# Reordering the start of a 1-core AdaLN kernel: the first mixer group's norms, table load and modulation

## The chip, the cores and the metric

The kernel runs on one core of a Trainium2 chip. The metric is device time in microseconds (us), the median of three runs. The engines are named as in the profile: PE (TensorE matmul, PEld its weight loads), DVE (VectorE), ACT (ScalarE), POOL (GpSimd), SP (SyncE, which issues most transfers). PEclk is the granted clock of TensorE, which has two levels, 1.2 and 2.4 GHz.

## What is computed

Two AdaLN blocks over x of 2 x 1024 x 128 (float32), each "norm, modulate, mixer, gated add, norm, modulate, feed-forward, gated add". Only the first mixer's start is touched:

```python
mod = (silu(c) @ wmod).reshape(2, 6, 1, -1)          # sa, ca, ga, sb, cb, gb
h = layernorm(x) * (1 + ca) + sa
r  = sigmoid(h @ W_r.T + b_r)
ek = exp(h @ W_k.T + b_k);  v = h @ W_v.T + b_v
td, g = exp(b_td), exp(global_decay)
# scan over time
sa = ek_t*v_t + td*sa;  sb = ek_t + td*sb
wkv = (g*ek_t*v_t + sa) / (g*ek_t + sb + EPS)
# then a spiking membrane over r_t*wkv: mem, reset, spk
x = x + ga * spikes
...                                                   # local attention x2 layers, LRU, mixture of experts
```

## The kernel before, in words

The 2048 tokens lie in four groups of 512 columns (`NG = 4`, `g` from 0 to 3), channels on the 128 partitions. Each engine has its own instruction list, written out by hand in order; the only links are semaphores, so an instruction that waits holds everything behind it on its own engine.

For a mixer group g the chain of work is this:

- DVE `mixer_stats(g)`: mean and variance of four token tiles (L865, L868), then L870 and L871, which signals `ln_var`.
- POOL `ln_rstd`: reciprocal root by a power (L632, `rst`) and L633 (`nmr`), which signals `ln_rstd`.
- ACT `mixer_norm(g)` (L374, four activations into `lnx`), signals `ln_norm`.
- PE `mixer_turn(g)` turns x (L1330 on `big`) and `ln_t2` turns `lnx` (L1330 on `lnx`). ACT `mixer_x(g)` (L388) copies the first.
- ACT `mixer_out(g)` (L380) applies the modulation and writes `hsA`; for g = 0 it first waits for `mod_fin`.
- PE multiplies `hsA` by the k and v weights (L1383, L1386).
- ACT makes `ek` (L409, needs the Exp table), scales it by `sc[:,1:2]` (L412, for g = 0 waits for `sc_ready`), and makes `gek` (L414).
- DVE: L911 (`ek*v`, waits for both products and `ek_ready`), two scans (L917 for `sbb`, L919 for `sab`), L922, then the reciprocal L925. The reciprocal waits for `den_ready`, which POOL L683 signals: the sum of `gek` and `sbb`, which waits for `gek_ready` and `sb_ready` (end of L917).
- POOL after L683 of group 0: `rope_tables(0)`, four products (L642, L645), ahead of L683 of group 1.

After the four groups DVE runs the membrane passes until about 86 us; then come PE transposes, the norm and attention.

Off this chain: POOL computes the decays `sc` from `vec` with small powers (L653 to L658, which end with `sc_ready`), and L662 to L665 for the LRU. The modulation is Silu of c (ACT L365), twelve small products on PE (L1369), seven small instructions on DVE (from L887 on) that end with `mod_fin`. `warm(n)` issues n products of the identity with itself, two passes each (L1362), and their result is not used. `ident` and `vec` are the two transfers on ACT's queue (L360, L361), both counted on `ld_c`.

POOL runs the decays, then `ln_rstd` of groups 0 and 1, then L662 to L665, then `ln_rstd` of groups 2 and 3. `ln_stats` of group n waits for `ln_norm` of group n-2, since the buffers alternate.

Of the kernel before, what the change touches and what calls it, by code (L numbers as in the profile page):

```python
# [13 lines left out]
ACT = mybir.ActivationFunctionType  # L14
# [61 lines left out]
def program(nc, a, out):  # L76
    with ExitStack() as ctx:
        def sb(name, shape, dt=F32):
            return ctx.enter_context(nc.sbuf_tensor(name, shape, dt))
# [4 lines left out]
        def sem(name):  # L84
            return ctx.enter_context(nc.semaphore(name))


        ident = sb("ident", [P, P])
# [33 lines left out]
        tvec = big[:, 5, 0:T]  # L122

        ek, gek, ekv, sab, sbb, _, rsg = (big[:, i, :] for i in range(7))

        oT = big[:, 0:4, :]
# [52 lines left out]
        psT0 = ps("psT0", [P, GW])  # L179
        psT1 = ps("psT1", [P, GW])  # L180

        names = """ld_x0 ld_x1 ld_x2 ld_x3 ld_wm0 ld_wm1 ld_ew ld_c ld_wr ld_wa ld_wq ld_wl ld_lru ld_moe ld_out st_out
            init table edges mod_raw silu_c mod_mm mod_fin sc_ready
            ln_t1 ln_var ln_rstd ln_norm ln_t2 ln_out
            xT_fill xT_evac
# [9 lines left out]
        s = {n: sem(n) for n in names}  # L195
# [3 lines left out]
        def gsl(g):  # L199
            return slice(g * GW, (g + 1) * GW)  # L200

        def bof(g):
            return g // GPB
# [3 lines left out]
        def ln_no(stage, g):  # L207
            return stage * NG + g
# [22 lines left out]
        def out_bank(n):  # L231

            if n // NG == 1:
                return psO[:, 0, :]
            return psO[:, 1, :] if n >= 5 * NG and n % 2 == 0 else psT1[:, :]
# [10 lines left out]
        def out_before(n):  # L246

            return n if n < 5 * NG else n - 1
# [108 lines left out]

        @block.scalar
        def _(act):
            act.dma_start(ident[:, :], a["ident"]).then_inc(s["ld_c"], 16)  # L360
            act.dma_start(vec[:, :], a["vec"]).then_inc(s["ld_c"], 16)  # L361
            own = Steps(act, s["act_own"])

            act.wait_ge(s["ld_c"], 32)
            act.activation(silc[:, :], vec[:, V_C:V_C + 4], ACT.Silu).then_inc(s["silu_c"], 1)  # L365


            def ln_norm(n, src=None):
                act.wait_ge(s["ln_rstd"], n + 1)
                if n >= 2:  # L370
                    act.wait_ge(s["ln_t2"], n - 1)
                src = stat_bank(n) if src is None else src
                for k in range(TPG):
                    act.activation(lnx[:, n % 2, k, :], src[:, k, :], ACT.Identity, bias=nmr[:, n % 2, k:k + 1],  # L374
                                   scale=rst[:, n % 2, k:k + 1]).then_inc(s["ln_norm"], 1)


            def ln_out(n, dst, scale, bias):
                act.wait_ge(s["ln_t2"], n + 1)
                act.activation(dst, out_bank(n), ACT.Identity, bias=bias, scale=scale).then_inc(s["ln_out"], 1)  # L380


            def mixer_norm(g):
                ln_norm(ln_no(0, g), xt[:, g * TPG:(g + 1) * TPG, :])

            def mixer_x(g):
                act.wait_ge(s["xT_fill"], g + 1)
                act.activation(x_cm[:, gsl(g)], psT0[:, :], ACT.Copy).then_inc(s["xT_evac"], 1)  # L388

            def load_table(function):  # L390

                act.activation(sc[:, 9:10], half[:, 0:1], function).then_inc(s["table"], 1)

            def mixer_out(g):
                if g == 0:
                    act.wait_ge(s["mod_fin"], 1)
                b = bof(g)
                ln_out(ln_no(0, g), hsA[:, gsl(g)], mod[:, 0, CA, b:b + 1], mod[:, 0, SA, b:b + 1])

            mixer_norm(0)  # L400
            mixer_x(0)
            mixer_norm(1)
            act.wait_ge(s["init"], 2)
            load_table(ACT.Exp)
            mixer_out(0)
            for g in range(NG):

                act.wait_ge(s["kv_mm"], 2 * g + 1)
# [209 lines left out]
        def _(pool):  # L618
# [8 lines left out]
            def ln_rstd(n):  # L627

                pool.wait_ge(s["ln_var"], n + 1)
                if n >= 2:  # L630
                    pool.wait_ge(s["ln_norm"], TPG * (n - 1))
                own.one(pool.tensor_tensor(rst[:, n % 2, :], mv[:, n % 2, :, 1], half[:, 0:TPG], ALU.pow))  # L632
                pool.tensor_tensor(nmr[:, n % 2, :], nmean[:, n % 2, :], rst[:, n % 2, :], ALU.mult).then_inc(s["ln_rstd"], 1)  # L633
# [15 lines left out]

            pool.wait_ge(s["ld_c"], 32)
            own.one(pool.memset(fr[:, 0:1], float(np.e)))  # L653
            own.did(pool.tensor_tensor(sc[:, 0:1], fr[:, 0:1], vec[:, V_BTD:V_BTD + 1], ALU.pow))
            own.did(pool.tensor_tensor(sc[:, 2:3], fr[:, 0:1], vec[:, V_GD:V_GD + 1], ALU.pow))
            own.one(pool.tensor_scalar(fr[:, 1:2], vec[:, V_BTD:V_BTD + 1], 0.0, -T / 2, ALU.max, ALU.mult))
            own.one(pool.tensor_tensor(sc[:, 1:2], fr[:, 0:1], fr[:, 1:2], ALU.pow))
            pool.tensor_scalar(sc[:, 3:4], sc[:, 1:2], 1e-6, 0.0, ALU.mult, ALU.add).then_inc(s["sc_ready"], 1)  # L658
            ln_rstd(ln_no(0, 0))
            ln_rstd(ln_no(0, 1))  # L660
            for dst, src in ((4, V_NU), (5, V_TH), (6, V_GAM)):
                own.did(pool.tensor_tensor(sc[:, dst:dst + 1], fr[:, 0:1], vec[:, src:src + 1], ALU.pow))  # L662
            own.sync()
# [194 lines left out]
        def _(dve):  # L858
# [17 lines left out]
            def mixer_stats(g):  # L876

                dve.wait_ge(s[f"ld_x{g}"], 16)
                ln_stats(ln_no(0, g), xt[:, g * TPG:(g + 1) * TPG, :])

            mixer_stats(0)
            mixer_stats(1)
            dve.wait_ge(s["ld_c"], 32)
            def modulation(k, bank):

                dve.wait_ge(s[("mod_mm", "mod_raw")[k]], 1)
                own.one(dve.tensor_copy(mod[:, k, :, :], bank[:, 0:12].rearrange("p (k n) -> p k n", k=6)))  # L887
                own.did(dve.tensor_scalar(mod[:, k, CA::3, :], mod[:, k, CA::3, :], 1.0, None, ALU.add))
                gk = mod[:, k, GA::3, :]
                sgn, mag = modt[:, 0, :, :], modt[:, 1, :, :]  # L890
                own.did(dve.tensor_scalar(sgn, gk, 0.0, 2.0, ALU.is_ge, ALU.mult))
                own.one(dve.scalar_tensor_tensor(out=mag, in0=gk, scalar=-1.0, in1=gk, op0=ALU.mult, op1=ALU.max))
                own.one(dve.tensor_scalar(sgn, sgn, -1.0, None, ALU.add))
                own.one(dve.scalar_tensor_tensor(out=gk, in0=mag, scalar=0.25, in1=sgn, op0=ALU.max, op1=ALU.mult))
                dve.tensor_copy(zero[:, 0:1], mod[:, k, 0, 0:1]).then_inc(s["mod_fin"], 1)
# [430 lines left out]
        def _(pe):  # L1326
            mm = pe.matmul
            def four(dst, src):
                for k in range(TPG):
                    i = pe.transpose(dst[:, k * P:(k + 1) * P], src(k), ident[:, :])  # L1330
                return i
# [6 lines left out]
            def ln_t2(n):  # L1338
                pe.wait_ge(s["ln_norm"], TPG * (n + 1))
                if n:  # L1340
                    pe.wait_ge(s["ln_out"], out_before(n))
                four(out_bank(n), lambda k: lnx[:, n % 2, k, :]).then_inc(s["ln_t2"], 1)


            pe.wait_ge(s["ld_c"], 32)

            def mixer_turn(g):
                pe.wait_ge(s[f"ld_x{g}"], 16)
                if g:
                    pe.wait_ge(s["xT_evac"], g)  # L1350
                four(psT0, lambda k: xt[:, g * TPG + k, :]).then_inc(s["xT_fill"], 1)
# [7 lines left out]
            def warm(times):  # L1359

                for _ in range(times):
                    mm(psO[:, 0, 0:P], ident[:, :], ident[:, :], start=True, stop=True)  # L1362

            mixer_turn(0)
            pe.wait_ge(s["silu_c"], 1)
            def modulation(k, bank):
                pe.wait_ge(s[f"ld_wm{k}"], 16)
                for j in range(6):
                    i = mm(bank[:, j * 2:j * 2 + 2], wmod[:, k, j * P:(j + 1) * P],  # L1369
                           silc[:, 2 * k:2 * k + 2], start=True, stop=True)  # L1370
                i.then_inc(s["mod_mm"], 1)

            warm(6)
            modulation(0, psQK[:, 0, :])
            warm(4)

            ln_t2(ln_no(0, 0))
            pe.wait_ge(s["ld_wr"], 16)
            for g in range(NG):
                pe.wait_ge(s["ln_out"], ln_no(0, g) + 1)  # L1380
# [479 lines left out]
```

## Time and profile before

| what | us |
|---|---|
| median of 3 runs (lowest, highest) | 576.92 (576.17, 577.79) |
| the profiled execution: its own time | 577.64 |
| the profiled execution: its span | 575.7 |
| busy in the span: PE, DVE, ACT, POOL | 487.1, 445.6, 347.6, 309.3 |
| mean granted PE clock | 0.948 |

All instruction times below come from the profiled execution and count from the start of its span. A timeline row reads: start, duration, engine, line, operation, output <- inputs, count, and in brackets how long the engine was idle before it and what released it. Merged rows (x4) give the start of the first and the time to the end of the last.

### The profile page before, as it was taken

To read this page: it belongs to the slowest core of one execution; us is meant where nothing else is said; L and a number is where in the kernel's file an instruction comes from. 1 tells how busy PE (TensorE), PEld (TensorE's weight loads), DVE (VectorE), ACT (ScalarE), POOL (GpSimd) and SP (SyncE) were. 2 spreads that over 40 slices of the span, in tenths; PEclk is the share of its full clock that TensorE was granted. 3 is DMA by queue.
4 is the path that set the end of the run, shared out by engine and by line. 5 is a ranking of instruction groups with operands and counts; after the bars stand their busy time and mean duration, and the time that the engine had idled before them with its cause. 6 is when DMAs were issued, how large, how long until landed. Compare 5 with 4: busy or idle time off the path is not lost. (4 is left out here: it accounts for less than half of the span.)

```text
span 575.7 us, 11716 instructions
## 1 busy us (share of the span) xinstructions
PE 487.1 (85%) x4006; PEld 310.9 (54%) x4006; DVE 445.6 (77%) x1197; ACT 347.6 (60%) x1001; POOL 309.3 (54%) x252
## 2 busy tenths in 40 slices
PE   6541026689999999999989999999999999999995
PEld 5311013357777776543457777776544445667774
DVE  5899998998999995546799999996455687457775
ACT  4861002579999997643469999997647526533331
POOL 5651002788888888576878888885010275110000
PEclk9995558889999999999989999999999999999999
DMA  8400002011111112100021111111000000000000
GB/s 292 148 1 1 1 1 71 3 38 40 37 38 36 37 35 45 49 1 1 0 84 39 39 38 40 38 40 29 10 1 1 0 2 0 1 0 20 20 18 20
DMA packets 14194, 18.89 MB, mean 33 GB/s; under 512 B 2187, under 2 KB 8629, under 8 KB 14005
## 3 DMA queue, kind: packets, MB, share of 16 engines
q1 hardware_dynamic: 13844, 18.04, 11.7%
q8 instruction: 33, 0.54, 0.4%
q14 instruction: 29, 0.23, 0.1%
q10 hardware_dynamic: 288, 0.08, 0.1%
HBM read 8.94 MB, written 1.05 MB: 17 GB/s over the span
## 5 line engine op out<-in xcount | busy, mean ns | idle before, releaser
L500 ACT ACTIVATE prob<-psS,nmx 128x128 f32<-128x128 f32 x256 | 89.9, 377 | 19.2 <-DVE nmx L1064 19.2
L775 POOL TENSOR_TENSOR rn<-ssq,half 128x16 f32<-128x16 f32 x32 | 93.4, 2917 | 5.7 <-DVE ssq L1050 2.7
L632 POOL TENSOR_TENSOR rst<-mv,half 128x4 f32<-128x4 f32 x24 | 25.9, 1078 | 125.1 <-DVE mv L871 65.3
L767 POOL TENSOR_TENSOR ra<-ra,rb 128x512 f32<-128x512 f32 x64 | 80.5, 1278 | 0.6 <-DVE rb L1032 0.6
L1404 PE MATMUL psQK<-wqkv,hsA 128*128 128x512 f32 x128 | 63.4, 620 | 2.6 <-ACT sq L435 1.4
L500 ACT ACTIVATION_READ_ACCUMULATOR prob<-psS,nmx 128x1 f32 x256 | 55.4, 216 | 0.0
L1029 DVE TENSOR_TENSOR ra<-psQK,rope 128x512 f32<-128x512 f32 x64 | 43.9, 686 | 6.6 <-PE psQK L1404 5.9
L783 POOL TENSOR_TENSOR qkn<-ra,rn 128x512 f32<-128x512 f32 x32 | 33.3, 1042 | 28.0 <-DVE qkn L1058 28.0
L1330 PEld LDWEIGHTS psT<-ident,qkn 128*128 128x128 f32 x256 | 30.3, 143 | 26.4 <-issue 15.3
L1032 DVE TENSOR_TENSOR rb<-psQK,rope 128x512 f32<-128x512 f32 x64 | 43.6, 681 | 0.0
L1064 DVE TENSOR_REDUCE nmx<-psS 128x4 f32<-128x512 f32 x64 | 41.1, 684 | 3.1 <-PE psS L1495 3.1
L614 ACT ACTIVATE gel<-psQK 128x512 f32<-128x512 f32 x32 | 19.1, 597 | 39.7 <-PE psQK L1704 39.7
L1330 PE MATMUL psT<-ident,qkn 128*128 128x128 f32 x256 | 35.0, 279 | 8.2 <-DVE qkn L1058 6.9
L374 ACT ACTIVATE lnx<-psS,nmr,rst 128x128 f32<-128x128 f32 x20 | 7.5, 456 | 55.7 <-POOL nmr L633 55.7
L1043 DVE TENSOR_REDUCE ssq<-sq 128x8 f32<-128x512 f32 x64 | 40.9, 677 | 0.2
L474 ACT ACTIVATE pT<-psT 128x512 f32<-128x512 f32 x64 | 36.3, 649 | 4.4 <-PE psT L1330 4.4
L1515 PE MATMUL psO<-vAB,pT 128*64 128x64 f32 x1024 | 36.9, 225 | 1.6 <-ACT pT L474 1.6
L1330 PEld LDWEIGHTS psT<-ident,prob 128*128 128x128 f32 x256 | 29.8, 141 | 15.0 <-issue 14.4
L1515 PEld LDWEIGHTS psO<-vAB,pT 128*64 128x64 f32 x1024 | 32.4, 138 | 7.4 <-ACT pT L474 4.7
L1447 PE MATMUL psO<-wqkv,hsA 128*128 128x512 f32 x64 | 36.4, 651 | 0.0
L1404 PEld LDWEIGHTS psQK<-wqkv,hsA 128*128 128x128 f32 x128 | 23.8, 204 | 22.3 <-issue 22.3
L1410 PE MATMUL psO<-masks,identb 128*128 128x512 bf16 x12 | 4.5, 553 | 35.7 <-DVE vAB L943 35.7
(236 smaller groups left out, 1201.3 us busy)
## 6 DMA issues: line engine op xcount, KB each, us to landing
vAB<-vAB SPq DMA_DIRECT2D x62, 128.0 KB, 2.2
wqkv<-in_wqkv SPq DMA_DIRECT2D x2, 768.0 KB, 7.7
big<-in_x SPq DMA_DIRECT2D x4, 256.0 KB, 4.9
ropeb<-in_rope SPq DMA_DIRECT2D x1, 1024.0 KB, 6.5
big<-in_ew SPq DMA_DIRECT2D x2, 512.0 KB, 4.4
out<-big SPq DMA_DIRECT2D x4, 256.0 KB, 2.3
wmod<-in_wmod SPq DMA_DIRECT2D x2, 384.0 KB, 6.3
w<-in_w SPq DMA_DIRECT2D x2, 341.0 KB
```

The source lines that it names most:

```text
L474: act.activation(pT[:, 4 * hb:4 * hb + 4, :], four((psT0, psT1)[hb]), ACT.Copy).then_inc(s["pT_evac"], 1)
L500: act.activation(prob[:, k, :], psS[:, hb, c * P:(c + 1) * P], ACT.Exp, bias=nmx[:, k:k + 1], accum_out=sums[:, n % 2, k:k + 1]).then_inc( ...
L767: pool.tensor_tensor(o, o, rb[:, r], ALU.add).then_inc(s["sum_" + name], 1)
L775: pool.tensor_tensor(rn[:, :], ssq[:, :], half[:, :], ALU.pow).then_inc(s["rn_ready"], 1)
L1029: dve.tensor_tensor(heads(o), heads(psQK[:, part, :]), rope[:, at8, 2 * part, :].unsqueeze(1).to_broadcast([P, H, DH]), ALU.mult).then_inc ...
L1032: dve.tensor_tensor(rb[:, r].rearrange("p (h a d) -> p h a d", h=H, a=2), psQK[:, part, :].rearrange("p (h a d) -> p h a d", h=H, a=2)[:, ...
L1043: dve.tensor_reduce(ssq[:, 8 * part:8 * part + 8], heads(sq[:, part * INNER:(part + 1) * INNER]), AX.X, ALU.add).then_inc(s["ssq_" + name], 1)
L1064: dve.tensor_reduce(nmx[:, 4 * hb:4 * hb + 4], psS[:, hb, :].rearrange("p (h k) -> p h k", h=4), AX.X, ALU.max, negate=True).then_inc(s["n ...
L1330: i = pe.transpose(dst[:, k * P:(k + 1) * P], src(k), ident[:, :])
L1404: mm(psQK[:, part, :], hsA[:, tile(i)], wqkv[:, part * INNER:(part + 1) * INNER], start=True, stop=True).then_inc(s[name + "_mm"], 1)
L1447: mm(psO[:, 1, :], hsA[:, tile(i)], wqkv[:, 2 * INNER:3 * INNER], start=True, stop=True).then_inc(s["v_fill"], 1)
L1515: j = mm(psO[64 * w:64 * w + 64, 0, h * DH:(h + 1) * DH], pT[:, slot(h), 64 * w:64 * w + 64], (vA, vB)[w][:, u, h * DH:(h + 1) * DH], star ...
```

## The change

POOL's first two norm powers go ahead of the decays. ACT loads the Exp table right after Silu, and the order "norm 0, x 0, norm 1, table, out 0" becomes "table, norm 0, x 0, out 0, norm 1". `ident` gets its own semaphore, `ld_id`, so PE waits for it alone and the others wait for `vec` alone. PE's warming products are 3 ahead of the first turn, 1 behind the modulation and 2 behind `ln_t2`, in place of 6 and 4.

```diff
-            act.dma_start(ident[:, :], a["ident"]).then_inc(s["ld_c"], 16)
+            act.dma_start(ident[:, :], a["ident"]).then_inc(s["ld_id"], 16)
             act.dma_start(vec[:, :], a["vec"]).then_inc(s["ld_c"], 16)
...
-            act.wait_ge(s["ld_c"], 32)
+            act.wait_ge(s["ld_c"], 16)
...
+            act.wait_ge(s["init"], 1)
+            load_table(ACT.Exp)
             mixer_norm(0)
             mixer_x(0)
+            mixer_out(0)
             mixer_norm(1)
-            act.wait_ge(s["init"], 2)
-            load_table(ACT.Exp)
-            mixer_out(0)
...
-            pool.wait_ge(s["ld_c"], 32)
+            ln_rstd(ln_no(0, 0))
+            ln_rstd(ln_no(0, 1))
+            pool.wait_ge(s["ld_c"], 16)
             own.one(pool.memset(fr[:, 0:1], float(np.e)))
...
             pool.tensor_scalar(sc[:, 3:4], sc[:, 1:2], 1e-6, 0.0, ALU.mult, ALU.add).then_inc(s["sc_ready"], 1)
-            ln_rstd(ln_no(0, 0))
-            ln_rstd(ln_no(0, 1))
...
-            dve.wait_ge(s["ld_c"], 32)
+            dve.wait_ge(s["ld_c"], 16)
...
-            pe.wait_ge(s["ld_c"], 32)
+            pe.wait_ge(s["ld_id"], 16)
...
+            warm(3)
             mixer_turn(0)
             pe.wait_ge(s["silu_c"], 1)
...
-            warm(6)
             modulation(0, psQK[:, 0, :])
-            warm(4)
-
+            warm(1)
             ln_t2(ln_no(0, 0))
+            warm(2)
             pe.wait_ge(s["ld_wr"], 16)
```

## Rows read from the trace of the kernel before

**Rows 1.** The page's 40 slices of 14.4 us: TensorE's granted clock in tenths.

```profile
PEclk9995558889999999999989999999999999999999
```

**Rows 2.** Timeline of DVE, first and second group of the mixer.

```profile
17.93 0.76 DVE L911 SCALAR_TENSOR_TENSOR psO<-psO,vec,big 128x512 f32<-128x512 f32 x1 [2.43 <-ACT big L412]
...
21.76 3.34 DVE L925 RECIPROCAL big<-big 128x512 f32<-128x512 f32 x1
...
25.73 1.63 DVE L917 TENSOR_TENSOR_SCAN big<-sc,big 128x512 f32<-128x512 f32 x1
```

**Rows 3.** Timeline of ACT up to the first `ek`.

```profile
9.24 1.65 ACT L374 ACTIVATE lnx<-big,nmr,rst 128x128 f32<-128x128 f32 x4 [3.75 <-POOL nmr L633]
...
12.93 1.28 ACT L392 ACT_TABLE_LOAD   x1
...
14.33 0.76 ACT L380 ACTIVATE hsA<-psT,mod 128x512 f32<-128x512 f32 x1
16.37 0.69 ACT L409 ACTIVATE big<-psS,vec 128x512 f32<-128x512 f32 x1 [1.28 <-PE psS L1383]
17.09 0.72 ACT L412 ACTIVATE big<-big,sc 128x512 f32<-128x512 f32 x1
```

**Rows 4.** Timeline of PE up to the first k product.

```profile
6.22 2.77 PE L1362 MATMUL psO<-ident 128*128 128x128 f32 x12
8.78 2.56 PE L1369 MATMUL psQK<-silc,wmod 128*128 128x2 f32 x12
...
13.04 1.06 PE L1330 MATMUL psT<-ident,lnx 128*128 128x128 f32 x4
15.23 1.10 PE L1383 MATMUL psS<-hsA,wrkv 128*128 128x512 f32 x2 [1.13 <-ACT hsA L380]
```

**Rows 5.** One line's instructions: 512-column float32 products, ns min/median/max.

```profile
L1404 PE MATMUL psQK<-wqkv,hsA x128: 591/593/1062, 98.3 to 385.2; 128*128 128x512 f32 x128
```

**Rows 6.** Timeline of POOL: decays, norm powers, denominator, rope tables.

```profile
5.38 0.10 POOL L653 MEMSET fr<- 128x1 f32 x1 [3.66 <-DMA vec<-in_vec]
...
7.90 1.03 POOL L632 TENSOR_TENSOR rst<-mv,half 128x4 f32<-128x4 f32 x1
...
9.16 1.01 POOL L632 TENSOR_TENSOR rst<-mv,half 128x4 f32<-128x4 f32 x1
...
10.40 1.60 POOL L662 TENSOR_TENSOR sc<-fr,vec 128x1 f32<-128x1 f32 x3
...
12.36 0.55 POOL L665 TENSOR_TENSOR sc<-fr 128x1 f32<-128x1 f32 x1
...
20.09 1.27 POOL L683 TENSOR_TENSOR big<-big 128x512 f32<-128x512 f32 x1 [3.22 <-DVE big L917]
...
24.99 1.29 POOL L645 TENSOR_TENSOR rope<-ropeb,qks 128x512 f32<-128x512 f32 x1
```

**Rows 7.** Timeline of DVE: ends of the first two statistics, start of the third.

```profile
5.73 0.16 DVE L871 TENSOR_SCALAR mv<-mv 128x4 f32<-128x4 f32 x1
...
7.89 0.16 DVE L871 TENSOR_SCALAR mv<-mv 128x4 f32<-128x4 f32 x1
...
12.47 0.87 DVE L865 BATCH_NORM_STATS2 st<-big 128x6 f32<-128x128 f32 x4
```

**Rows 8.** Timeline: issue of `ident` on ACT's queue.

```profile
0.72 0.43 ACTq L360 DMA_DIRECT2D ident<-in_ident  x1
```

**Rows 9.** Page, part 6: `ident`, KB and us to landing.

```profile
ident<-in_ident ACTq DMA_DIRECT2D x1, 64.0 KB, 2.7
```

**Rows 10.** The tile `wmod`: both halves, us from issue to landing.

```profile
DMA to landing us min/median/max: 4.3/6.3/8.4
```

**Rows 11.** Timeline of DVE and POOL in a later stage: a scan beside small powers.

```profile
473.26 1.02 POOL L632 TENSOR_TENSOR rst<-mv,half 128x4 f32<-128x4 f32 x1 [0.23 <-DVE mv L871]
473.75 1.21 DVE L1219 TENSOR_TENSOR_SCAN z<-sc,ra 128x512 f32<-128x512 f32 x1
474.35 0.60 POOL L633 TENSOR_TENSOR nmr<-nmean,rst 128x4 f32<-128x4 f32 x1
```

More of the change, by code:

```diff
@@ L180, in program @@
         psT1 = ps("psT1", [P, GW])
-        names = """ld_x0 ld_x1 ld_x2 ld_x3 ld_wm0 ld_wm1 ld_ew ld_c ld_wr ld_wa ld_wq ld_wl ld_lru ld_moe ld_out st_out
+        names = """ld_id ld_x0 ld_x1 ld_x2 ld_x3 ld_wm0 ld_wm1 ld_ew ld_c ld_wr ld_wa ld_wq ld_wl ld_lru ld_moe ld_out st_out
             init table edges mod_raw silu_c mod_mm mod_fin sc_ready
```

## The prediction, written before the changed kernel ran

> **What bounds the kernel now.** I read the page first. The 40 slices [rows 1] show TensorE's granted clock near its upper level for the first three slices (43 us), then at half for three (the membrane passes, where PE has nothing to do), and near the upper one again almost to the end. So the start is one stage, the membrane the next, and attention and the rest follow; the change touches the first alone.
>
> Then the timeline of DVE. The first mixer product L911 starts at 17.93 after 2.43 us of waiting for ACT's L412 [rows 2]. From there DVE has no wait until the membrane is over: the reciprocal L925 at 21.76 runs 3.34 us, and the next group's work stands right behind it. What reaches L911 of group 0 earlier reaches the end of the membrane earlier, as long as nothing else becomes late in the groups. The reader should look for such a thing in the scan L917 of group 1: it took 1.63 us [rows 2], against 1.21 of a scan of the same size that ran free [rows 11]. POOL's last rope table L645 ran from 24.99 to 26.28 [rows 6], the scan ended at 27.36, so it really began its 1.2 us when POOL let go. DVE works here on a beat that POOL gives: POOL's denominator L683 ends at D = 20.09 + 1.27 = 21.36 [rows 6], four tables follow, and the scan ends at D + 6.0. After that, group 1's chain is DVE's again. **The gain of the change is by how much D moves**, not by how much L911 moves.
>
> What sets L911 before: ACT waits for the norm power until 9.24 (3.75 us), loads the table at 12.93 and writes `hsA` only at 14.33 [rows 3]; PE has turned `lnx` by 14.10 [rows 4].
>
> **Part 1, the norm power first.** Statistics of group 0 end at 5.73 + 0.16 = 5.89 [rows 7], yet POOL's power starts at 7.90, since the decays (from 5.38) stand ahead [rows 6]. In the changed kernel it starts at about 5.98. ACT's L374 came 9.24 - 7.90 = 1.34 later, so it starts at 7.32 and, at 1.65, ends at 8.97 [rows 3]. That is 1.92 earlier.
>
> **Part 2, the table load.** It costs 1.28 [rows 3] wherever it stands. Now it follows Silu, which is released by `vec` like POOL's L653 at 5.38 [rows 6], so it is over by 7.1, in ACT's wait for the norm power. It costs nothing with 0.2 us to spare; without that cover its excess would move L374 one for one. Identity and Copy follow the Exp load now too (L380 behind it at 14.33), so they need no other.
>
> **Part 3, PE.** `ident` is there at 0.72 + 2.7 = 3.4 [rows 8, 9]. Six warming products at 2.77/12 = 0.23 [rows 4] end at 4.8, the turn of x at 5.9, and the modulation, which began at 8.78 only because of the warming ahead of it, runs from 5.7 to 8.45 (2.56 and the first weight load) [rows 4]; its weights, second on SP's queue, need at least 4.3 from their issue [rows 10], some 5.5 at the earliest. DVE's seven instructions end with 12.47 - 11.34 = 1.13 after the products [rows 4, 7]: 9.6. `ln_t2` waits for `lnx` at 8.97 and ends 1.1 later, 10.1; `mod_fin` lies beneath it. ACT is free by then (between norm and L380 stands the x copy alone, shorter than L409's 0.69 for as many columns), so L380 runs from 10.15 to 10.9 and the k product starts 0.14 behind it, at 11.05, in place of 15.23 [rows 3, 4].
>
> **Part 4, the clock.** The page grants the upper level in the first slice [rows 1], but the rows say otherwise: the `lnx` turn takes 1.06 for four, and the k product that follows 1.10 for two [rows 4], while the same kind of float32 product elsewhere takes 593 ns at the full and 1062 at half clock [rows 5]. So PE ran at half from its first work, which `vec` released near 5.3 like POOL's [rows 6], until 14.10, 8.8 us with hardly a wait, and at full from 15.23. In the changed kernel PE starts at 3.4, waits before `ln_t2`, and has much less warming behind the modulation; 11.05 is 7.6 after its start. I take half clock for group 0: spacing 0.85, the k pair ends at 11.05 + 0.85 + 1.06 = 13.0 and the v pair 1.7 later, 14.7. L409 runs from 13.05, L412 from 13.77 to 14.49 [rows 3], so the v product decides and L911 starts at 14.8. At full clock both are there by 14.0. Norm 1, now behind L380 on ACT, runs from 10.9 to 12.5 beneath the product; at full clock it would be last, by 0.3.
>
> **Part 5, who is late next.** The decays begin 1.24 behind the second power (9.16 to 10.40) [rows 6]. The second power waits for its statistics at 8.05 [rows 7] and starts at 8.14; the decays run from 9.38 for 7.90 - 5.38 = 2.52 and `sc_ready` comes at 11.9, 1.9 ahead of L412: no cost. But L662 to L665 follow for 2.51 [rows 6], to 14.4, and only then the powers of groups 2 and 3, which had been done long before L683 and now stand right ahead of it. DVE's statistics (under 2.2 a group, 5.89 to 8.05) [rows 7] start at 9.6 and, for group 3, which waits for norm 1, at 12.5: they end ahead of 14.7 and do not delay L911. POOL: L632 from 14.49 to 15.5, then L633 at 15.6. L911 takes 0.76, so the scan L917 of group 0 runs from 15.6 to 16.8 beside it. The late stage shows what that does: L633 started inside a scan took 0.60 until that ended, not 0.20 [rows 11]. So L633 ends near 16.75, L632 and L633 of group 3 take 1.24 more, and L683 runs from 18.0 to D = 19.25. Before, L683 had waited 3.22 for the scan [rows 6]; now POOL has 1.15 of work behind the scan's end. D moves by 21.36 - 19.25 = 2.1, where L911 moves by 3.1.
>
> The bounds of this unseen overlap: on the good side L633 slips through and group 3's power too, which leaves 14.5 + 2 x 1.24 + 1.27: D = 18.2 (gain 3.1, the whole of L911's); on the bad side the first power is caught by the scan as well and all three steps stand behind 16.7: D = 20.4 (gain 1.0). The nearest row is the blocked L633, so I take 2.1.
>
> In these rows the power at 473.26 was running when the scan started, and the scan took its usual 1.21 [rows 11]: it was not held up. The Trainium skill (SBUF — State Buffer, section Who interferes with whom) says that of GpSimd and a VectorE instruction with two SBUF inputs the one that issues first has the shared port pair for its whole instruction, and the other blocks. By that rule the scan would also wait for the powers, for up to 1.0, L922 would be the later one for the reciprocal, and the gain would be about 2.0; the trace disagrees for a power of four columns.
>
> **The sum.** 2.1 earlier at group 1's scan, nothing more after it: DVE continues without a wait, then PE. The profiled execution took 577.64 (span 575.7), which gives 575.5 (span 573.6); the median of the runs, 0.72 lower, gives 576.92 - 2.1 = **574.8**.
>
> **Rivals.** *(a) Full shift.* The clock is up by 11.05, or POOL gets through beside the scan. With the clock up, L911 starts at 14.0 and the scan at 14.8; L632 is in flight already, L633 is blocked to 16.0, and D = 16.0 + 1.24 + 1.27 = 18.5, a gain of 2.8; with nothing blocked 3.1, where POOL's own work is the bound even if L911 gains more. Time 573.8 to 574.1. For it: PE starts its work 1.9 us earlier. Against: less warming just ahead of the product.
> *(b) Eaten behind the membrane.* The shift arrives, but PE comes to attention in another state of its clock: one row of 1062 ns in the middle of full-speed ones [rows 5] shows that clock changes occur there. At half clock, each us of PE work at full speed costs one more, so some 0.4 to 2 us of such work eat the gain down to nothing: 575.2 to 576.9. The three runs' spread of 1.6 says that such amounts occur anyway.
> *(c) Slower.* The same mechanism at the first attention tiles at full length: PE stays at half clock for work of over 3.8 us at full speed: at 1062 - 593 = 0.47 a product [rows 5], eight slow products of this kind on the path. It eats the 2.1 and adds 1.7. Time 578.7 and more. For it: nothing that the change does; against: PE is loaded there by 12 products of `keep_clock` that wait for DVE and shift with it.
> *(d) It does nothing.* The decays are late instead (`sc_ready` behind 14.5). It would need 2.6 us more on POOL ahead of it.
>
> **How the numbers follow.** About 0.3% (1.7 us) is what a measurement of this kernel can tell from no change. Forecast case 0.50 (574.8, own range 574.0 to 575.6), (a) 0.20, (b) and (d) 0.24, (c) 0.06. Faster by over 0.3% (below 575.2): 0.7 of the forecast case, nearly all of (a), some of (b): 0.60. Within: 0.33. Slower: 0.07. The range takes the forecast, (a) at 573.8 less half the spread of the runs (573.0), and most of (b), up to 576.3.
>
> **What would show it.** Right: L374 at 7.3; L1383 at 11.0 with two products in nearly 2 us; L911 near 14.8 with ACT or PE as its releaser; POOL's L632 and L633 stretched or shifted under the scan; L683 ending near 19.2 with no idle time before it, and DVE idle for some 0.5 us before L925 with POOL as its releaser; L917 of group 1 long still. Wrong: L1383's pair in 1.1 us, L683 waiting for DVE as before (gain 3 or more), or the membrane's end 2 us earlier and the total not.

## The result and the profile after

The changed kernel took 574.68 us (median of 9 runs, 573.36 to 575.87); the kernel before took 576.92 (576.17 to 578.87, also 9 now). The ratio is 0.9946, with a 95% interval of 0.9935 to 0.9957: 3.1 us faster by the ratio (2.5 to 3.7), 2.2 by the two medians. Forecast were 574.8 and 2.1. Later the same changed kernel gave 574.61 and a ratio of 0.9947 (0.9932 to 0.9962). Both intervals lie wholly on the faster side of 0.3%. The time was met within 0.1 us, but the forecast gain of 2.1 lies below the interval of the gain by the ratio.

The profiled execution has a span of 573.3. Timeline of the changed kernel, ACT, to be laid beside [rows 3]:

```profile
4.70 1.28 ACT L392 ACT_TABLE_LOAD   x1
...
7.39 1.65 ACT L374 ACTIVATE lnx<-big,nmr,rst 128x128 f32<-128x128 f32 x4 [1.20 <-POOL nmr L633]
8.95 0.58 ACT L388 ACTIVATE x_cm<-psT 128x512 f32<-128x512 f32 x1
10.32 0.78 ACT L380 ACTIVATE hsA<-psT,mod 128x512 f32<-128x512 f32 x1 [0.79 <-PE psT L1330]
...
13.32 0.69 ACT L409 ACTIVATE big<-psS,vec 128x512 f32<-128x512 f32 x1 [0.69 <-PE psS L1383]
14.04 0.72 ACT L412 ACTIVATE big<-big,sc 128x512 f32<-128x512 f32 x1
```

The table load now lies in ACT's wait for the norm power, with 1.2 us to spare; the norm starts 1.85 earlier and the modulated output 4.0 earlier. PE, beside [rows 4]:

```profile
3.47 1.65 PE L1362 MATMUL psO<-ident 128*128 128x128 f32 x6 [3.47 <-DMA ident<-in_ident]
...
5.76 2.56 PE L1370 MATMUL psQK<-silc,wmod 128*128 128x2 f32 x12
...
9.10 1.11 PE L1330 MATMUL psT<-ident,lnx 128*128 128x128 f32 x4
...
11.24 2.05 PE L1383 MATMUL psS<-hsA,wrkv 128*128 128x512 f32 x2 [0.17 <-ACT hsA L380]
13.08 1.89 PE L1386 MATMUL psO<-hsA,wrkv 128*128 128x512 f32 x2
```

The k pair takes 2.05 where it took 1.10 before: half clock, so of the 4.0 won at L380 one is given back here, and DVE's L911 is now released by the v pair (L1386), not by ACT. POOL, beside [rows 6]:

```profile
7.85 1.02 POOL L632 TENSOR_TENSOR rst<-mv,half 128x4 f32<-128x4 f32 x1 [0.49 <-DVE mv L871]
...
14.16 1.02 POOL L632 TENSOR_TENSOR rst<-mv,half 128x4 f32<-128x4 f32 x1
15.26 0.20 POOL L633 TENSOR_TENSOR nmr<-nmean,rst 128x4 f32<-128x4 f32 x1
15.41 1.01 POOL L632 TENSOR_TENSOR rst<-mv,half 128x4 f32<-128x4 f32 x1
16.50 0.52 POOL L633 TENSOR_TENSOR nmr<-nmean,rst 128x4 f32<-128x4 f32 x1
17.16 1.27 POOL L683 TENSOR_TENSOR big<-big 128x512 f32<-128x512 f32 x1
```

And DVE, beside [rows 2]:

```profile
15.00 0.76 DVE L911 SCALAR_TENSOR_TENSOR psO<-psO,vec,big 128x512 f32<-128x512 f32 x1 [0.70 <-PE psO L1386]
15.79 1.23 DVE L917 TENSOR_TENSOR_SCAN big<-sc,big 128x512 f32<-128x512 f32 x1
...
18.83 3.34 DVE L925 RECIPROCAL big<-big 128x512 f32<-128x512 f32 x1
...
22.80 1.63 DVE L917 TENSOR_TENSOR_SCAN big<-sc,big 128x512 f32<-128x512 f32 x1
...
44.26 0.11 DVE L933 MEMSET vst<- 128x64 f32 x1
```

POOL's denominator L683 ends at D = 18.43, 2.93 earlier than before; the scan that it needs and POOL's last L633 both end at 17.02, so POOL's new backlog costs nothing yet, and the reciprocal at 18.83 shows no wait. That is not what was forecast (D = 19.25 and a wait of some 0.5); e10 below shows the forecast case. The scan of group 1 ends at 24.43 = D + 6.00, as in the kernel before (21.36 and 27.36). The membrane starts at 44.26. In the kernel before:

```profile
47.19 0.11 DVE L933 MEMSET vst<- 128x64 f32 x1
```

2.93 earlier. The span shrank by 2.4 only. Some of the difference goes at once behind the membrane: the turn of `lnx` and the first attention product, before and after:

```profile
95.75 0.65 PE L1330 MATMUL psO<-ident,lnx 128*128 128x128 f32 x4 [0.88 <-ACT lnx L374]
...
98.34 1.95 PE L1404 MATMUL psQK<-wqkv,hsA 128*128 128x512 f32 x4 [1.11 <-DVE hsA L1013]
```

```profile
92.86 0.85 PE L1330 MATMUL psO<-ident,lnx 128*128 128x128 f32 x4
...
95.65 1.95 PE L1404 MATMUL psQK<-wqkv,hsA 128*128 128x512 f32 x4 [1.30 <-DVE hsA L1013]
```

The product comes 2.69 earlier: the turn of `lnx` took 0.85 for four in place of 0.65, so it began at half clock, and the norm's chain passes through it.

### The profile page after: what moved, and what is told of

Same layout as the page of the kernel before. It is cut to its first block and busy times, and to the rows that moved or that the text cites. A ratio compares the mean times of both kernels' runs of the same rounds, so it can differ in the third digit from the quotient of the medians.

```text
span 573.3 us, 11700 instructions
## 1 busy us (share of the span) xinstructions
PE 489.5 (85%) x3998; PEld 310.4 (54%) x3998; DVE 446.1 (78%) x1197; ACT 348.0 (61%) x1001; POOL 309.9 (54%) x252
## 5 line engine op out<-in xcount | busy, mean ns | idle before, releaser
L632 POOL TENSOR_TENSOR rst<-mv,half 128x4 f32<-128x4 f32 x24 | 25.9, 1080 | 128.8 <-DVE mv L871 70.3
L374 ACT ACTIVATE lnx<-psS,nmr,rst 128x128 f32<-128x128 f32 x20 | 7.5, 458 | 55.7 <-POOL nmr L633 55.7
L1330 PEld LDWEIGHTS psT<-ident,prob 128*128 128x128 f32 x256 | 29.8, 141 | 14.8 <-issue 14.1
```

## The experiments

All of them edit the changed kernel. "L911" is the start of the first L911, D the end of the first L683 (POOL's denominator). "Membrane" is the start of DVE's L933 in the trace, which no later clock can disturb; "rest" is the span less it. Ratios are to the kernel before, run on the same chip between the others. All intervals overlap that of the changed kernel, except those of e2 and e5; where the text goes by a smaller difference, it rests on the trace. Of the change's four parts the separate semaphore of `ident` was undone in none of the runs, so its share is not known.

| run | median | ratio (95%) | L911 | D | membrane | span | rest |
|---|---|---|---|---|---|---|---|
| before | 576.92 | 1 | 17.93 | 21.36 | 47.19 | 575.7 | 528.5 |
| changed | 574.68 | 0.9946 (0.9935 to 0.9957) | 15.00 | 18.43 | 44.26 | 573.3 | 529.0 |
| e1 POOL back | 575.36 | 0.9958 (0.9946 to 0.9971) | 15.82 | 19.25 | 45.07 | 574.1 | 529.0 |
| e2 ACT back | 576.40 | 0.9976 (0.9967 to 0.9985) | 17.13 | 20.56 | 46.61 | 575.4 | 528.8 |
| e3 PE back | 574.99 | 0.9966 (0.9951 to 0.9982) | 14.50 | 18.82 | 44.63 | 573.3 | 528.7 |
| e11 the same, once more | 576.07 (1 run) | | 17.07 | 20.49 | 46.32 | 574.2 | 527.9 |
| e4 LRU powers late | 574.53 | 0.9946 (0.9933 to 0.9958) | 15.00 | 18.43 | 44.25 | 572.1 | 527.9 |
| e5 LRU powers before L683 | 576.15 | 0.9981 (0.9971 to 0.9990) | 14.90 | 20.05 | 45.86 | 574.3 | 528.4 |
| e6 no warming | 574.56 | 0.9953 (0.9940 to 0.9967) | 14.95 | 19.42 | 45.23 | 573.8 | 528.6 |
| e7 warming on zeros | 574.38 | 0.9956 (0.9943 to 0.9969) | 15.05 | 18.49 | 44.31 | 572.3 | 528.0 |
| e8 no collisions | 573.73 | 0.9936 (0.9923 to 0.9949) | 14.86 | 19.34 | 43.96 | 572.8 | 528.8 |
| e9 e4 and e8 | 573.35 | 0.9928 (0.9914 to 0.9942) | 14.47 | 17.89 | 42.87 | 571.9 | 529.0 |
| e10 changed, again | 574.61 | 0.9947 (0.9932 to 0.9962) | 14.41 | 18.89 | 44.71 | 572.7 | 528.0 |

**e1, POOL's part undone.**

```diff
-            ln_rstd(ln_no(0, 0))
-            ln_rstd(ln_no(0, 1))
             pool.wait_ge(s["ld_c"], 16)
...
             pool.tensor_scalar(sc[:, 3:4], sc[:, 1:2], 1e-6, 0.0, ALU.mult, ALU.add).then_inc(s["sc_ready"], 1)
+            ln_rstd(ln_no(0, 0))
+            ln_rstd(ln_no(0, 1))
```

> The changed kernel with POOL's part alone undone (decays ahead of the first two norm powers). My theory: the start is one chain, POOL's power, ACT's norm, PE's turn, ACT's modulated output, PE's products, DVE; a part undone moves all behind it. The decays take 2.5 us from vec's landing (4.4 to 5.3), so L632 starts at 7.0 to 7.9 in place of 6.05, L374 at 8.3 to 9.2, L911 at 15.9 to 16.9 in place of 15.00, and 0.9 to 1.9 us of the 2.9 are lost: ratio to the kernel before 0.996 to 0.998. Rival, the three parts help each by itself and this one is a third: 1.0 us lost, and undoing either of the others loses 1.0 too.

The power started at 7.00, ACT's norm at 8.34 in place of 7.39, L911 at 15.82: 0.8 lost at the membrane, 0.7 by the ratios. That is less than the 1.9 by which the power was late in the kernel before, since `vec` landed before 4.4 here and at 5.3 there. By the intervals it can't be told from a third of the gain, nor from no loss; the 0.8 rests on the trace.

**e2, ACT's order undone.**

```diff
-            act.wait_ge(s["init"], 1)
-            load_table(ACT.Exp)
             mixer_norm(0)
             mixer_x(0)
-            mixer_out(0)
             mixer_norm(1)
+            act.wait_ge(s["init"], 1)
+            load_table(ACT.Exp)
+            mixer_out(0)
```

> The changed kernel with ACT's order alone undone: norm 0, x 0, norm 1, table load, output 0. My theory: L374 starts at 7.4 as in the changed kernel, but L380 comes behind norm 1 (1.6) and the load (1.3, then 0.2), at 12.6 in place of 10.32. If PE's clock is still at half for the first products, 2.3 us are lost and the ratio to before is 0.998 to 0.9995; if the clock has come up by 13.5, the v pair takes 0.95 less and 1.3 are lost. Rival (parts add by thirds): 1.0 lost, ratio 0.9965.

L380 started at 12.44, the products were still at half clock (2.04), and 2.35 were lost at the membrane: 2.13 at L911 and at D, as the chain says for half clock, and 0.22 in the scan of group 3, which took 2.02 here and 1.80 in the changed kernel. By the ratios 1.7 are lost (0.9976 against 0.9946). The thirds are out: with this part alone undone, most of the gain is gone.

**e3 and e11, PE's order undone.**

```diff
-            warm(3)
             mixer_turn(0)
...
+            warm(6)
             modulation(0, psQK[:, 0, :])
-            warm(1)
+            warm(4)
             ln_t2(ln_no(0, 0))
-            warm(2)
```

> The changed kernel with PE's order alone undone (no warming ahead of the first turn, six products ahead of the modulation, four behind it); ident keeps its own semaphore. My theory: the turn waits for x at 4.3, the warming runs to 8.0, the modulation to 10.6, four more products to 12.4, and ln_t2 ends at 13.3 in place of 10.2: L380 3.0 later. The first products then run at full clock as in the kernel before (two in 1.1 in place of 2.05), which gives 0.9 back: 2.1 to 2.9 lost, ratio 0.998 to 1.000, almost the whole gain. Rival (thirds): 1.0 lost, ratio 0.9965.

Here my number was wrong. PE in the trace of e3:

```profile
5.23 2.62 PE L1362 MATMUL psO<-ident 128*128 128x128 f32 x12
7.69 1.40 PE L1369 MATMUL psQK<-silc,wmod 128*128 128x2 f32 x12
8.95 1.14 PE L1362 MATMUL psO<-ident 128*128 128x128 f32 x8
9.92 0.60 PE L1330 MATMUL psT<-ident,lnx 128*128 128x128 f32 x4
11.55 1.10 PE L1382 MATMUL psS<-hsA,wrkv 128*128 128x512 f32 x2 [1.02 <-ACT hsA L380]
```

The clock came up at the modulation (1.40 for twelve, not 2.56) and everything behind ran at full. L911 was earlier than in the changed kernel, at 14.50. The 0.4 us lost at the membrane came from POOL: the last norm power began 0.10 behind the scan's start and took 1.93 in place of 1.01, so D was 18.82 and DVE waited 0.44 for it. But the twelve times lie in two heaps, seven from 574.1 to 575.2 and five from 577.2 to 577.4, so the ratio in the table, a middle between heaps, describes neither. One more trace of the same program, on another chip:

> The kernel with PE's order undone, for one more trace: its twelve times fell into two heaps, 574.1 to 575.2 (seven) and 577.2 to 577.4 (five). The first trace was of the lower heap: the clock came up at about 7.8, the modulation took 1.40 in place of 2.56 and L380 started at 10.62. Theory: in the upper heap the clock stays at half until behind ln_t2, L380 starts near 13.3 as first expected, and the time is 2.5 to 3 higher. If this trace is of the upper heap it shows that; if of the lower one, it repeats 10.6.

```profile
5.19 2.77 PE L1362 MATMUL psO<-ident 128*128 128x128 f32 x12
7.75 2.56 PE L1369 MATMUL psQK<-silc,wmod 128*128 128x2 f32 x12
10.18 2.05 PE L1362 MATMUL psO<-ident 128*128 128x128 f32 x8
12.02 1.06 PE L1330 MATMUL psT<-ident,lnx 128*128 128x128 f32 x4
14.11 1.10 PE L1382 MATMUL psS<-hsA,wrkv 128*128 128x512 f32 x2 [1.03 <-ACT hsA L380]
```

The same program, the same starts to 0.1 us, and the clock stays at half until `ln_t2` is through: L380 at 13.19 against 10.62, as first expected, L911 at 17.07. Its time of 576.07 lies between the heaps, and the heaps' medians (574.64 and 577.31) are 2.7 apart where the two membranes are 1.7 apart (44.63 and 46.32). So that the clock makes the two heaps is not shown; it explains at most a part of their distance. In the upper heap the gain is almost gone (the kernel before took 577.79 on that chip), in the lower one nothing is lost (e4, with PE's order as in the changed kernel, took 574.53 there).

The Trainium skill (TensorE: Matmul & The Clock Gate, Part 1) says that the chip's look at PE's activity is not aligned with the kernel's start, so that the point of change varies from run to run, by 500 ns either way. These two traces agree that it varies, and not on the size: at full clock before the modulation was over in one, at half until behind `ln_t2` in the other, over 4 us later.

**e4 and e5, how late POOL may be.** e4 moves the LRU powers (L662 to L665) behind `current(2)`; e5 moves them right ahead of L683. Both take them out here:

```diff
-            for dst, src in ((4, V_NU), (5, V_TH), (6, V_GAM)):
-                own.did(pool.tensor_tensor(sc[:, dst:dst + 1], fr[:, 0:1], vec[:, src:src + 1], ALU.pow))
-            own.sync()
-            own.one(pool.tensor_scalar(fr[:, 2:3], sc[:, 4:5], -1.0, 0.0, ALU.mult, ALU.add))
-            own.one(pool.tensor_tensor(sc[:, 7:8], fr[:, 0:1], fr[:, 2:3], ALU.pow))
             for g in range(2, NG):
                 ln_rstd(ln_no(0, g))
```

In e5 the five lines stand right behind this loop, in e4 behind `current(2)`.

> The changed kernel with the three LRU powers and the two instructions behind them (2.5 us of POOL) moved behind the last current, where POOL idles. The prediction said POOL would be late for L683 and set the gain. If that holds on this chip, L683 ends up to 1 us earlier and the time falls by up to 0.5 us against the changed kernel. The trace of the changed kernel says otherwise: L683 ends at 18.43, and DVE reaches the reciprocal at 18.83 without waiting for POOL. By it nothing changes: ratio to before 0.9946 within 0.001, L925 at 18.8.

> The changed kernel with the LRU powers (2.5 us) moved from ahead of the norm powers of groups 2 and 3 to behind them, right ahead of L683. This makes POOL late on purpose. Theory (POOL's lateness at L683 costs one for one beyond a margin of 0.4 us): the powers of group 3 wait for their statistics at 14.3 and end at 15.5, the LRU powers run beside the scan to 18.0 or later, L683 ends at 19.3 or more in place of 18.43, DVE waits 0.5 to 1.5 ahead of L925, and this is lost: ratio to before 0.9955 to 0.997. Rival, POOL is no limit of this stage at all: ratio 0.9946 and no wait ahead of L925.

e4 changed nothing: POOL now idles for 1.52 ahead of L683, which starts at 17.16 as in the changed kernel (D = 18.43, membrane 44.25, same ratio). So in this execution the backlog was free. e5 made POOL late:

```profile
18.07 0.75 DVE L922 SCALAR_TENSOR_TENSOR big<-psO,sc,big 128x512 f32<-128x512 f32 x1
20.08 3.35 DVE L925 RECIPROCAL big<-big 128x512 f32<-128x512 f32 x1 [1.26 <-POOL big L683]
...
24.06 1.98 DVE L917 TENSOR_TENSOR_SCAN big<-sc,big 128x512 f32<-128x512 f32 x1
```

D rose by 1.62 to 20.05, DVE waits 1.26, the next scan ends at 26.04 = D + 5.99, and the membrane starts 1.60 later. By the ratios 2.0 us are lost (1.4 to 2.5 on e5's own interval). So the rule of the prediction, the membrane moves with D, holds one for one here.

**e6 and e7, the warming products.** e6 takes out all three `warm` calls ahead of the first k product; e7 puts seven on zeros at the very start in place of the three:

```diff
+            pe.wait_ge(s["init"], 2)
+            for _ in range(7):
+                mm(psO[:, 0, 0:P], kT2[:, 0, 0:2, :].rearrange("p w t -> p (w t)"), kT2[:, 1, 0:2, :].rearrange("p w t -> p (w t)"), start=True, stop=True)
             pe.wait_ge(s["ld_id"], 16)
...
-            warm(3)
```

> The changed kernel without any warming product ahead of the first k product (the output of these products isn't used). Theory: with the changed kernel's short warming the first four products run at half clock anyway, so nothing is lost there: L1383's pair in 2.05 again, L911 at 15.0, ratio 0.9946 within 0.001. If the clock then stays low for group 1 too there is slack of some 2 us on ACT before DVE. Rival (the warming products carry the gain): L911 or a later group's L911 waits for PE, and 0.5 us or more are lost.

> The changed kernel with seven products on zeros of kT2 from 1.75 us on in place of the three on the identity, so that PE works without a pause from 1.8 to 8.9. Theory: where the clock has come up by 11.2 the first pairs take 1.1 and 1.0 in place of 2.05 and 1.89, L911 starts at 14.3 to 14.5 (behind ACT's norm 1 and DVE's third and fourth statistics) and POOL becomes the late one: at most 0.5 us gained, ratio 0.9937 to 0.9946. Rival: zeros don't bring the clock up, half clock as in the changed kernel, ratio 0.9946 and L911 at 15.0.

e6: L1383's pair in 2.05 at 11.16, L911 at 14.95 against 15.00, so in this trace the changed kernel's warming does nothing for these products. The membrane's 45.23 is POOL's doing: the second norm power started at 8.72 (the second part of x had landed late), and DVE waited 0.59 for L683. e7, PE:

```profile
1.77 3.35 PE L1347 MATMUL psO<-kT 128*128 128x128 f32 x14 [1.77 <-POOL kT L621]
4.92 0.77 PE L1330 MATMUL psT<-ident,big 128*128 128x128 f32 x4
5.52 1.43 PE L1372 MATMUL psQK<-silc,wmod 128*128 128x2 f32 x12
6.81 0.47 PE L1365 MATMUL psO<-ident 128*128 128x128 f32 x2
9.12 1.11 PE L1330 MATMUL psT<-ident,lnx 128*128 128x128 f32 x4 [1.84 <-ACT lnx L374]
```

Both theories missed. Products on zeros do bring the clock up: it rose during the turn of x at 4.92 (0.77 for four, 1.06 in the changed kernel), and the modulation took 1.43. Then PE waits 1.84 us for ACT's norm, with twelve products of two columns and one warming product ahead of it, and at 9.12 the clock is at half again. The granted clock on record says the same: 0.92 from 7 to 9 us and 0.50 from 9 to 14. Nothing gained at L911 (15.05).

**e8, DVE's scans kept clear of POOL.**

```diff
-            def rope_tables(l):
+            def rope_tables(l, cs=range(4)):
...
                 if g == 0:
                     pool.wait_ge(s["ld_wa"], 64)
-                    rope_tables(0)
+                    rope_tables(0, range(3))
                 if g == 1:
                     quotient(0)
+                    rope_tables(0, range(3, 4))
...
                     current(1)
-                    quotient(2)
+            quotient(2)
             current(2)
```

> The changed kernel with two of POOL's works moved away from DVE's scans: the fourth rope table behind the quotient of group 0 instead of ahead of the denominator of group 1, and the quotient of group 2 behind the last denominator. Theory (a POOL product with two inputs in SBUF holds up a scan that starts beside it): L917 of group 1 takes 1.23 in place of 1.63 and that of group 3 1.23 in place of 1.8, together 0.9 to 1.0 us earlier at the membrane: ratio to before 0.993 (0.992 to 0.994). Rival: odd groups' scans are longer because their start value is read from memory, and nothing changes: 0.9946.

```profile
19.38 3.35 DVE L926 RECIPROCAL big<-big 128x512 f32<-128x512 f32 x1 [0.60 <-POOL big L683]
...
23.36 1.28 DVE L918 TENSOR_TENSOR_SCAN big<-sc,big 128x512 f32<-128x512 f32 x1
...
37.49 1.28 DVE L918 TENSOR_TENSOR_SCAN big<-sc,big 128x512 f32<-128x512 f32 x1
```

The two scans take 1.28 (lines are one lower in this kernel), against 1.63 and 1.8: POOL's products held them up. The 0.05 or 0.06 left against the scans of groups 0 and 2 (1.22 and 1.23) may be the start value, which only groups 1 and 3 read from memory. The ratio is 0.001 (0.6 us) better than the changed kernel's, well inside both intervals; what is shown is the trace, in which the membrane starts 0.30 earlier though the second part of x landed late here too and POOL was late by 0.60.

**e9 and e10, both moves on POOL beside the changed kernel.**

> The changed kernel with both moves on POOL: the LRU powers behind the last current, and the fourth rope table and the quotient of group 2 moved away from DVE's scans. Theory: with the powers gone POOL can't be late at L683 of group 0 even when the second part of x lands late (in the last run DVE waited 0.60 there), and the scans of groups 1 and 3 take 1.28 in place of 1.63 and 1.8. So DVE has no wait from L911 to the membrane, which starts at 43.3 in place of 44.26 (43.96 with the scans alone mended): ratio to before 0.9925 to 0.9935. Rival: the scans alone carry it, ratio 0.9936 as in the last run.

> The changed kernel itself once more, on the same chip as the kernel that carries both of POOL's moves. Its first median lay 2.2 below the kernel before, its interval of ratios at 2.5 to 3.7. Expected from the traces: 2.9 us at the membrane, less up to 0.6 in executions in which the second part of x lands late and POOL is late for L683: ratio 0.9950 (0.9940 to 0.9960). Rival, the margin was never touched and the rest of the program gives nothing back: 0.9945 or lower.

e9: no wait on DVE, membrane at 42.87, 573.35 against 574.61 for e10 on the same chip: 1.26 us better than the changed kernel, ratio to before 0.9928. One of e10's six times lies among e9's, the other five above all of them. Its membrane is 0.4 earlier than I said, with the clock up a little sooner in this execution (k pair 1.68). Against e10, whose k pair took 1.67, the membrane is 1.84 earlier: the first reciprocal starts 0.63 earlier (18.30 and 18.93, where DVE had waited 0.61), the scan of group 1 is 0.70 shorter (1.98 there) and that of group 3 0.52. e10 shows the collision that the prediction described. POOL and DVE:

```profile
14.20 1.02 POOL L632 TENSOR_TENSOR rst<-mv,half 128x4 f32<-128x4 f32 x1
15.29 1.13 POOL L633 TENSOR_TENSOR nmr<-nmean,rst 128x4 f32<-128x4 f32 x1
16.38 1.01 POOL L632 TENSOR_TENSOR rst<-mv,half 128x4 f32<-128x4 f32 x1
17.46 0.20 POOL L633 TENSOR_TENSOR nmr<-nmean,rst 128x4 f32<-128x4 f32 x1
17.61 1.28 POOL L683 TENSOR_TENSOR big<-big 128x512 f32<-128x512 f32 x1
```

```profile
15.20 1.22 DVE L917 TENSOR_TENSOR_SCAN big<-sc,big 128x512 f32<-128x512 f32 x1
...
18.93 3.35 DVE L925 RECIPROCAL big<-big 128x512 f32<-128x512 f32 x1 [0.61 <-POOL big L683]
```

L633 starts 0.09 behind the scan and takes 1.13 until that ends; the steps behind it follow; D = 18.89 and DVE waits 0.61. L911 is 0.59 earlier than in the first trace and the membrane 0.45 later. The second part of x was not late here (second power at 7.89, against 7.85 in the first trace); it was the sooner clock that brought the scan ahead of POOL's L633.

## Why the prediction was right

- **Norm power first** (7.32 for L374, 1.9 earlier): 7.39. Right.
- **Table load hidden**: right, with 1.2 us of cover and not 0.2, since `vec` landed 0.9 earlier in this execution.
- **PE's restart** (L380 at 10.15, product at 11.05): 10.32 and 11.24. Right.
- **Half clock for group 0** (L911 at 14.8): pair in 2.05, L911 at 15.00. Right. It was not a sure thing: in e9 and e10 the pair took 1.68 and 1.67, the clock coming up in the middle of it, and the v pair ran at full (1.02). No trace of this order had the k pair at full clock throughout.
- **POOL late at L683** (D = 19.25, gain 2.1): the mechanism exists, its size was too large, and in the first trace it cost nothing. In the first trace D = 18.43, since the second part of x landed earlier (second power at 7.85, not 8.14) and L911 came 0.2 later; group 3's power slipped in ahead of the scan and only the last L633 was caught (0.52). In e10 the first L633 was caught as written, but because L911 came at 14.41, not at 14.8; D = 18.89. e6 and e8, with the same POOL order up to L683, show D = 19.42 and 19.34 and the wait of 0.6. So the gain at the membrane is 2.93 in one execution and 2.48 in another of the same kernel. D was put 0.4 to 0.8 too late. That POOL's lateness costs DVE is shown by e5 and e10, and the scan's end at D + 6.0 held in the traces of both kernels and of e1 to e7, e10 and e11 to 0.02 (with the fourth table moved away it is D + 5.30 in e8 and D + 5.66 in e9). A small reading was off: the scan of group 1 ended 1.08 behind the end of the last table (26.28 and 27.36), not 1.2, so some 0.2 of it had been done beside POOL.
- **The total** (574.8, measured 574.68): close in part by luck. The gain of 2.1 was too small, below the 2.5 to 3.7 of the ratio and the 2.93 and 2.48 at the membrane; taken from a median of the kernel before (576.92) that lies below those of later series (577.13 to 577.79), it still gave the right time.
- **Behind the membrane**: the rest of the span lies between 527.9 and 529.0 in the traces, with no order by kernel. The first trace of the changed kernel happens to have 529.0 and that of before 528.5. This scatter of 1.1 is as large as the differences between most of the experiments. It is rival (b) in its small form: it adds or takes half a microsecond, and did not eat the gain. Only the start of it, the 0.2 at the turn of `lnx`, is traced to the clock here. The 1062 ns that the prediction read as one row is the longest of 128; the trace of before has at least four such products between 111 and 123 us, so the clock changes there without the edit too.

How the three parts share the 2.9 us: undone one at a time they cost 0.8 (POOL), 2.35 (ACT) and, for PE, 2.1 where the clock stayed at half. Where it came up early (e3), PE's part was worth nothing: L911 was even 0.5 earlier, and the 0.4 lost was POOL's. The three don't add up to the gain; they lie one behind another on one chain, and each undone part delays what the others made early.

The Trainium skill (SBUF — State Buffer, Who interferes with whom) says that a VectorE instruction with two SBUF inputs contends with a GpSimd instruction that reads SBUF, over a shared port pair that it calls an exclusive lock. That the first one has the pair for its whole instruction it says in its line on VectorE's 2-port modes; the prediction took it for the scan too. That POOL's small instruction blocks when it starts behind the scan: the traces agree (1.13 and 0.52 in place of 0.20). That the scan blocks when POOL's power is in flight first: the traces disagree for the 128x4 power, L632 ran from 15.41 when the scan started at 15.79, and it took 1.23. For a 512-column product they agree that the scan is held up (1.62 to 2.02 in place of 1.28).

## What to carry to other kernels

Ask for each engine that is made earlier which other engine feeds the step behind it: here L911 moved by 2.9 us and POOL, which had waited 3.2 us at that place, was left with almost no margin. An engine can be held up by another without showing a wait, visible only as an instruction that is longer than its like; moving two such neighbours apart, with the move of the small powers, gave 1.3 us more. And where a stage's time depends on when a transfer lands or when the clock rises, take the trace of a second execution before naming the step that decides.

## What the runs showed of the hardware

- The granted clock of both kernels reads 1.00 in the first 14 us, but transposes take 1.06 to 1.12 us for four there and 0.60 later. At the start durations show the clock and the record doesn't; in e7, where the clock fell early, the record shows it (0.50 from 9 to 14 us).
- PE's clock came up behind products on zeros (e7, during the turn at 4.92, after a start at 1.77) and had fallen again at 9.12, behind two-column products, one warming product and a wait of 1.84.
- Two executions of one program, on two chips, whose PE work starts within 0.1 us of each other differ by 2.6 us at L380, by the clock (e3 and e11).
- A power of 128x4 on POOL costs 1.01 and one of 128x1 0.55. The one of 128x4 that was running when a scan began (15.41 and 15.79, changed kernel) neither delayed it nor was delayed; begun 0.10 behind the scan's start it took 1.93 (e3):

```profile
15.39 1.93 POOL L632 TENSOR_TENSOR rst<-mv,half 128x4 f32<-128x4 f32 x1
```
